# Causal attention with relative bias: heads' values in one PSUM bank, division moved behind the weighing, four-row score tiles, next job's bias and maximum ahead of norm work

## The reference, cut to what matters

```python
q, k, v = heads_split(x @ Wq), heads_split(x @ Wk), heads_split(x @ Wv)
q = q * cos + _rotate_half(q) * sin
k = k * cos + _rotate_half(k) * sin
scores = jnp.einsum('bhqd,bhkd->bhqk', q, k) / sqrt(HD) + bias
scores = jnp.where(causal, scores, jnp.float32(-1000000000.0))
attn = jax.nn.softmax(scores, axis=-1)
ctx = jnp.einsum('bhqk,bhkd->bhqd', attn, v)
return ctx.transpose(0, 2, 1, 3).reshape(b, s, d) @ Wo
```

## Time and profile before

| | us |
|---|---|
| median of 3 runs (2390.05 to 2390.89) | 2390.89 |
| the profiled execution's own time | 2393.39 |
| its span | 2391.5 |
| PE busy | 2271.0 (95%) |
| DVE busy | 1760.3 (74%) |
| POOL busy | 1595.7 (67%) |
| ACT busy | 1380.1 (58%) |

### The profile page before, as it was taken

The page is one execution under the profiler, slowest core; times in us unless marked ns, Lnnn a source line. Parts: engine busy times, 40 slices in busy tenths (PEclk is TensorE's granted clock), DMA queues, the critical chain, the costliest instruction groups (busy, mean ns, idle before and its releaser), DMA issues.

```text
span 2391.5 us, 81638 instructions
## 1 busy us (share of the span) xinstructions
PE 2271.0 (95%) x34944; PEld 1573.3 (66%) x34944; DVE 1760.3 (74%) x2707; ACT 1380.1 (58%) x2778; POOL 1595.7 (67%) x931
## 2 busy tenths in 40 slices
PE   7789999999999999999999999999987888889998
PEld 5456666666666666666666666666655666657776
DVE  3678888888888788878887888888846888853332
ACT  2256666666666666666666666666644666643442
POOL 1298888988898889888988888898833132201111
PEclk9799999999999999999999999999987999989999
DMA  4011112111221112211121112111121000000000
GB/s 116 3 38 36 32 34 67 44 34 31 60 53 33 32 36 60 52 32 36 44 59 40 36 32 61 49 37 32 33 77 48 1 1 2 1 1 1 5 5 9
DMA packets 77303, 83.91 MB, mean 35 GB/s; under 512 B 24964, under 2 KB 48786, under 8 KB 76946
## 3 DMA queue, kind: packets, MB, share of 16 engines
q1 hardware_dynamic: 76946, 78.70, 12.9%
HBM read 26.56 MB, written 1.07 MB: 12 GB/s over the span
## 4 chain that ended last, share of the span: by engine, by line
PE 63%; DVE 19%; issue 10%; ACT 5%; POOL 2%; SPq 0%; ACTq 0%; DMA 0%; POOLq 0%; DVEq 0%
PE bank L565 8%; PE bank L646 7%; PE bank L658 6%; DVE n L1288 5%; PE lnbank L586 4%; PE obank L635 4%; ACT qk L950 3%; PE bank L576 3%; PE obank L627 3%; PE sbank L602 3%; PE bank L666 3%; PE obank L612 3%; PE obank L868 2%; PE sbank L868 2%; PE sbank L791 2%
## 5 line engine op out<-in xcount | busy, mean ns | idle before, releaser
L1281 DVE TENSOR_TENSOR qk<-bank,tab 128x1024 f32<-128x1024 f32 x384 | 468.8, 1221 | 193.6 <-ACT qk L950 193.5
L1601 POOL TENSOR_TENSOR rn<-n2m,cst 128x16 f32<-128x16 f32 x192 | 562.5, 2930 | 16.0
L1597 POOL TENSOR_TENSOR qk<-qk 128x1024 f32<-128x1024 f32 x192 | 454.4, 2366 | 157.9 <-DVE qk L1281 157.9
L950 ACT ACTIVATE qk<-bank 128x512 f32<-128x512 f32 x384 | 226.9, 591 | 313.8 <-PE bank L565 313.8
L565 PE MATMUL bank<-wqk,xs 128*128 128x512 f32 x768 | 404.9, 609 | 1.4 <-ACT qT L968 0.7
L1605 POOL TENSOR_TENSOR qk<-qk,rn 128x1024 f32<-128x1024 f32 x192 | 365.1, 1902 | 28.2 <-POOL rn L1601 0.9
L576 PEld LDWEIGHTS bank<-cst,qk 128*128 128x128 f32 x1536 | 191.7, 141 | 215.1 <-issue 170.7
L576 PE MATMUL bank<-cst,qk 128*128 128x128 f32 x1536 | 232.3, 274 | 10.8 <-POOL qk L1605 10.7
L1288 DVE TENSOR_REDUCE n<-qk 128x16 f32<-128x1024 f32 x192 | 232.1, 1209 | 0.0
L1609 POOL TENSOR_TENSOR lnr<-lnv,cst 128x2 f32<-128x2 f32 (+1 forms) x76 | 54.2, 713 | 248.4 <-DVE lnv L1165 248.4
L586 PE MATMUL lnbank<-wv,xs 128*64 128x512 f32 x768 | 207.2, 618 | 0.0
(11 more groups left out here) (362 smaller groups left out, 4239.3 us busy)
## 6 DMA issues: line engine op xcount, KB each, us to landing
vp<-vp SPq DMA_DIRECT2D x672, 65.0 KB, 2.0
wqk<-in_L_ffn_Wqkv SPq DMA_DIRECT2D x24, 256.0 KB, 3.6
wv<-in_L_ffn_Wqkv SPq DMA_DIRECT2D x6, 512.0 KB, 4.2
wo<-in_L_ffn_Wo SPq DMA_DIRECT2D x6, 512.0 KB, 4.2
xs<-Z SPq DMA_DIRECT2D x48, 64.0 KB, 2.4
xs<-Z SPq DMA_DIRECT2D x48, 63.8 KB, 2.1
vp<-in_L_ffn_w SPq DMA_DIRECT2D x1, 2048.0 KB, 13.2
mw<-in_L_ffn_w SPq DMA_DIRECT2D x8, 256.0 KB, 6.8
```

The lines of the kernel that those rows point to most:

```text
L1281: tt(qk[:, both, :].rearrange("p o (h d) -> p o h d", d=DH), heads(bank[c % 2][:, :]).unsqueeze(1).broadcast_to([P, 2, PAIRS, DH]), table. ...
L1597: tt(direct, direct, swapped, ALU.add).then_inc(sum_done, 1)
L1601: tt(rn[:, m % 2, :], n2m[:, :], const("mhalf"), ALU.pow).then_inc(rn_done, 1)
```

## The change

- **Jobs**: a group y of three jobs now takes the heads y, y+4, y+8 and y+12. Their queries and keys lie in four different sets of 32 rows, so `qm` is masked only within 32 rows (four copies instead of 16, double-buffered), and the scores of a whole group are taken at once (`scores3`): eight products of 32 rows each, one bank of `quad` per set.
- **DVE**: `shift3` does addition and negated extreme in one instruction per head (scores are stored negated, and the exponential has scale -1), and it handles job m+1 in slot m, ahead of that slot's norm work.
- **Division**: exponentials are transposed and weighed undivided; row sums are kept for the batch (`dn`), inverted once (`invert`), spread over the features with a copy and two transposes (`spread_inverses`), and multiplied to the weighed values (`divide3`).
- **Values**: `placed` takes 32 columns around a head's 8 values (zeros beside them), so that 4 heads add up in one set of 32 rows: all 16 heads in one bank of 256 columns, in the order of features. The output projection is one product.
- **Order**: `sh` and `px` have three buffers; a step has 12 slots, the next batch's first group follows in slot 11; only the last step has four more. ACT does its norm work of slot m-1 in slot m, between its exponentials and its copy.
- **Loads**: bias in a buffer of its own, loaded behind layer 0 of the windowed stage; `mw2` in the memory of `kT` and `tab`; the output weights in one transfer, without zeroing.

```diff
-JOBS = [job for n in range(0, H, 4)
-        for job in ((0, range(n, n + 4)), (1, range(n, n + 2)), (1, range(n + 2, n + 4)))]
+JOBS = [job for y in range(4)
+        for job in ((0, range(y, H, 4)), (1, range(y, H // 2, 4)), (1, range(H // 2 + y, H, 4)))]
...
             layer(0, True, False)
+            sp.dma_start(bias[:, :, :], bass.AP(relu_dram.ap().tensor, 0, [[1, P], [384, H], [1, S]])).then_inc(rel_in, 16)
...
-            for half in range(2):
-                sp.dma_start(bias[half], bass.AP(relu_dram.ap().tensor, half * PAIRS * 384, [[1, P], [384, PAIRS], [1, S]]))\
-                    .then_inc(rel_in, 16)
...
             def out3(b):
-                pe.wait_ge(s3["ot"], 2 * b + 2)
-                for g in range(4):
-                    mm = nc.tensor.matmul(lnbank[:, 0:S], s3wo[:, g, :], s3ot[:, g, :], start=(g == 0), stop=(g == 3))
-                mm.then_inc(s3["y"], 1)
+                pe.wait_ge(s3["ot"], b + 1)
+                nc.tensor.matmul(lnbank[:, S:2 * S], s3wo, s3ot, start=True, stop=True).then_inc(s3["y"], 1)
...
+            def scores3(b, odd, y):
...
+                wait(pe, s3["mx"], NJ * b + 3 * y)
+                for r in range(2):
                     w = P * (r + 1)
+                    for g in range(4):
+                        rows = slice(WIN * g, WIN * g + WIN)
+                        mm = nc.tensor.matmul(quad[:, g, P * r:P * r + w], qm[rows, odd, y, r * P:r * P + P],
+                                              s3k[odd][rows, 0:w], start=True, stop=True)
+                mm.then_inc(s3["full"], 1)
+
+            def turn3(n):
+
+                pe.wait_ge(s3["px"], n + 1)
+                wait(pe, s3["pts"], n)
+                for q in range(4):
+                    mm = nc.tensor.transpose(bank[2][:, q * P:q * P + P], s3px[n % 3][:, q * P:q * P + P], ident)
+                mm.then_inc(s3["ptf"], 1)
...
+            def weigh3(n):
...
+                for kb in range(r + 1):
+                    for x, h in enumerate(heads):
+                        row, q = WIN * (h // 4), x * (r + 1) + kb
+                        mm = nc.tensor.matmul(bank[b % 2][row:row + WIN, lo:lo + P], placed(b % 2, kb, h),
+                                              pT[:, n % 2, q * P:q * P + P], start=(m == 0), stop=(y == 3 and kb == r),
+                                              skip_group_check=True)
...
             def step3(b, odd, next_batch, batch_before):
                 u = 3 * b + (LN_S3 + 1)
-                for m in range(NJ + 3):
-                    attend(b, odd, m)
+                for m in range(NJ if next_batch else NJ + 4):
+                    n = NJ * b + m
+                    if 2 <= n <= NJ * B + 1:
+                        turn3(n - 2)
+                    if m in (2, 5, 8):
+                        scores3(b, odd, m // 3 + 1)
+                    if m == NJ - 1 and next_batch:
+                        scores3(b + 1, 1 - odd, 0)
+                    if 3 <= n <= NJ * B + 2:
+                        weigh3(n - 3)
...
+                    if m == 3 and batch_before:
+                        spread_inverses(b - 1)
...
             def step3(b, odd, next_batch, batch_before):
                 u = 3 * b + (LN_S3 + 1)
-                for m in range(NJ + 3):
-                    attend(b, m)
+                for m in range(NJ if next_batch else NJ + 4):
+                    n = NJ * b + m
+                    if m < NJ:
+                        exps3(b, m)
+                    if batch_before:
+                        finish(b - 1, m - 1, u + 2 if next_batch else u)
                     if next_batch:
-                        prepare(b + 1, 1 - odd, m, u if batch_before else LN_S3 + 2)
...
+                        prepare(b + 1, 1 - odd, m - 1, u if batch_before else LN_S3 + 2)
+                    if m == 3 and batch_before:
+                        take_raw(b - 1)
...
+                    if 2 <= n <= NJ * B + 1:
+                        take_turned3(n - 2)
...
+            def shift3(b, m):
...
+                for x, h in enumerate(heads):
+                    last = nc.vector.tensor_tensor_reduce(out=s3sh[n % 3][:, x * w:x * w + w], in0=quad[:, h // 4, P * r:P * r + w],
+                                                          in1=bias[:, h, S - w:S], scale=-1.0, scalar=3e38, op0=ALU.add,
+                                                          op1=ALU.min, accum_out=mx[:, n % 3, x:x + 1])
+                last.then_inc(s3["mx"], 1)
...
+            def divide3(b):
+
+                dve.wait_ge(s3["rdw"], b + 1)
+                wait(dve, s3["y"], b)
+                tt(s3ot.rearrange("p (r t) -> p r t", r=2), s3raw.rearrange("p (r t) -> p r t", r=2),
+                   bank[b % 2][:, 0:S].rearrange("p (r t) -> p r t", r=2)[:, :, ::-1], ALU.mult).then_inc(s3["ot"], 1)
...
-                for m in range(NJ + 3):
-                    if m < NJ:
-                        attend(b, m)
-                    if 1 <= m <= NJ:
-                        normalise3(b, m - 1)
+                for m in range(NJ if next_batch else NJ + 4):
+                    if m < NJ - 1:
+                        shift3(b, m + 1)
+                    if m == NJ - 1 and next_batch:
+                        shift3(b + 1, 0)
+                    if m == 2 and batch_before:
+                        invert(b - 1)
```

More of the change, by code:

```diff
@@ L167, in build @@
         w1t = rotf[:, 512:1024]
-        mw2 = sb("mw2", [P, NE, 4, DIM])
+        bias = sb("bias", [P, H, S])
         sh = sb("sh", [P, 2, 512])
@@ L835, in _ @@
             step3(B - 1, 1, False, True)
-            for slot in range(9, 13):
-                finish(B - 1, slot, LN_S4 - 1, False)
+            for slot in range(8, 12):
+                finish(B - 1, slot, LN_S4 - 1)
             pe.wait_ge(ld_gate, 64)
@@ L1057, in finish @@
                 if slot == 9:
-                    act.wait_ge(s3["y"], b + 1)
-                    nc.scalar.copy(s3y, lnbank[:, 0:S]).then_inc(s3["ys"], 1)
-                if slot == 10:
                     ln_sq_act(S, u)
-            def attend(b, m):
-                if 2 <= m <= NJ + 1:
-                    act.wait_ge(s3["ptf"], NJ * b + m - 1)
-                    wait(act, s3["pv"], NJ * b + m - 3)
-                    nc.scalar.copy(pT[:, m % 2, :], bank[2][:, :]).then_inc(s3["pts"], 1)
-                if m < NJ:
-                    r, heads = JOBS[m]
-                    w = P * (r + 1)
-                    act.wait_ge(s3["mx"], NJ * b + m + 1)
-                    wait(act, s3["ptf"], NJ * b + m - 1)
-                    for n in range(len(heads)):
-                        last = nc.scalar.activation(px[:, m % 2, n * w:n * w + w], sh[:, m % 2, n * w:n * w + w], ACT.Exp,
-                                                    bias=mx[:, m % 2, n:n + 1], accum_out=dn[:, m % 2, n:n + 1])
-                    last.then_inc(s3["px"], 1)
@@ new lines, in exps3 @@
+            def exps3(b, m):
+                n = NJ * b + m
+                r, heads = JOBS[m]
+                w = P * (r + 1)
+                act.wait_ge(s3["mx"], n + 1)
+                wait(act, s3["ptf"], n - 2)
+                if m == 0:
+                    wait(act, s3["rdn"], b - 1)
+                for x, h in enumerate(heads):
+                    last = nc.scalar.activation(s3px[n % 3][:, x * w:x * w + w], s3sh[n % 3][:, x * w:x * w + w], ACT.Exp,
+                                                bias=mx[:, n % 3, x:x + 1], scale=-1.0,
+                                                accum_out=dn[:, b % 2, H * r + h:H * r + h + 1])
+                last.then_inc(s3["px"], 1)
```

214 lines of the change are left out of this document (101 added, 113 removed).

## The result

The kernel after takes 2307.32 us (median of 4 runs, 2304.07 to 2308.62) against 2390.47 for the kernel before, measured beside it: ratio 0.9651, 95% interval 0.9634 to 0.9668, so 83 us less where 49 were forecast. The profiled execution took 2308.0 us; its span is 2306.2.

A forecast was written before the change was run, and what follows sets the result against it. Bound: a serial walk through PE, DVE and ACT, per job before, per three-job group after. Savings of 41.5 (six middle steps), 7.4 (first) and 0.5 us (last) make 49.4: 2393.4 to 2344.0, adjusted to 2342; range 2310 to 2376.

The forecast's parts named there:

- The new walk: Second attention: serial path through PE, DVE and ACT once per group of three jobs, 7.44 us without norm work.
- The moved loads: Bias, weight tables and small loads issued elsewhere: forecast zero effect, up to 12 us if a spreading were late.
- ACT's wait for the maximum: Sign: ACT's largest idle time, before a four-head job's exponentials, ended by DVE, four times a step, about 2 us each.
- Scores of a group: PE's eight score products per group: 1.3 us, half the serial time, plus 0.15 until DVE starts; bounds 0.65 and 2.6.
- Fused operation: DVE's addition and maximum in one instruction per head: 0.38 us for 128 elements, 0.51 for 256.
- the copy between the exponentials: ACT's copy between four-head and two-head exponentials on each group's walk: 0.62 us.
- norm work on the walk: ACT's norm copies and squares, plus PE's projections outlasting the walk: 2.6 us a step.
- The first step: First of the second attention's eight steps: 7.4 us saved, with less norm work and a clock of 0.88 before.
- the last with its tail: Last step, 37.0 us with its drain against 35.97, and 1.5 us back from the projection: 0.5 us saved.
- Cheaper parts: Rival: scores overlap fourfold and the accumulator costs nothing, 2303 us, or some 2322 with only one; chance 25%.
- the double gain: Both cheap parts at once, fourfold score overlap and free accumulator output, 2303 us; left out of the range.
- norms and rotary, unchanged: DVE's norm and rotary work per step in the second attention: 8.0 us, taken as the same after the change.

The follow-up runs named there:

- e7: Changed kernel with one more 512-wide DVE addition in each slot of the six middle steps, behind the slot's other work: 2310.4 us.
- e14: Changed kernel with PE computing each group's eight score products twice, into the same places: 2329.1 us.
- e1: Changed kernel with all score products reading the first 32 rows, so none overlap and the output differs: 2402.35 us.
- e15: Changed kernel with each job's fused DVE operations done once more, ahead, into a scratch buffer: 2346.8 us.
- e5: Changed kernel with ACT's norm work issued in its own slot, not one slot later: 2353.1 us.
- e6: Changed kernel with DVE's shift of the next job behind the slot's norm work, not ahead of it: 2398.7 us.
- e13: Changed kernel with both order edits, those of e5 and e6, together: 2407.2 us.
- e9: Kernel of e6 with two unneeded 256-column PE products ahead of the weighing in nearly every slot: 2428.0 us.
- e10: Changed kernel with PE's scores ahead of the turn (2289.6 us), plus unneeded PE products behind the weighing in the first step's slots 3 to 11: 2295.0 us.

## Why the prediction was right and wrong

**Right: the bound and its kind.** The new walk, one per group of three jobs, and its members are in the trace as written: 32 waits of ACT for the maximum, 32 of DVE for scores. e7 shows that DVE's sum doesn't bind, e14 that scores stand on the walk one to one. The moved loads cost nothing: the stage starts 0.3 us earlier. No low clock remains between batches in the steady steps. ACT's wait for the maximum comes once a group as foretold, but is 1.2 us and not 2.

**Wrong: the size of two terms.** The forecast gave the walk 7.44 us per group without norm work; it is 6.26, 1.18 less. Two terms are 1.08 of that.

- *Scores of a group*: "I take half of the serial time, 1.3 us, plus 0.15 until DVE starts". Measured: 0.94 us, and 1.00 to DVE's start, 0.45 less. The step that failed is the choice between bounds: I discounted overlap because the row with small tiles had two row groups. Four row groups overlap 3.1-fold (0.94 against 2.88 us in e1), and the second pass of e14, 0.65 us, is just the forecast's bound for four at a time. The Trainium skill (TensorEngine Tiling (Array Packing), section Theoretical Speedup) gives up to 4x at 32 rows; the runs come near it, and not to half of the serial time.
- *Fused operation*: "I take ScalarE's extra of 0.18, as the nearest row: 0.38 and 0.51". Measured 0.21 and 0.34, the lower bound of 0.20 and 0.33. Shift to exponentials is 0.97 us, not 1.6: 0.63 less. The Trainium skill (VectorE: DVE Perf Modes, section Two Vector instructions with no wait between them) counts the accumulator's output as a second instruction; it is one in the trace, 0.08 us, but it starts with the next operation, and the pitch shows no time for it. A price carried over from another engine was the mistake.

The doubling runs say what an error in each term weighs: a microsecond of scores 1.0 (21.8 over 20.8), and one of the four-head job 1.0 in the two groups of e15 that are otherwise undisturbed. The 39.5 us of e15 as a whole are 1.5 times 32 times 0.84, but the two-head jobs were doubled too, and the clock fell; they are no weight of the one term.

1.08 us in each of four groups is 26 of the 29 us missed in six middle steps; the rest came from the copy between the exponentials (0.47 between starts, not 0.62) and from norm work on the walk, 2.3 us a step as against 2.6. The first step gave 12.2 in place of 7.4, the last with its tail 2.4 in place of 0.5. Together 36 us.

Both errors lay on the same side, and the prediction held them together as its rival *Cheaper parts*, "2303", at 25%; the measured 2307 is that case. The range left it out by its own words ("leaving out the double gain"). The two terms weren't independent coin throws of a quarter: each time I had chosen a dearer value, though the trace of before held a row for the near bound, for DVE and the earlier trace rows for PE.

**Not seen: what the order is worth.** The walk treated "ahead of norm work" as a place in a sum. e5, e6 and e13 cost 46, 91 and 100 us, far beyond the operations that change places, because each one queues a short operation behind a chain over three in-order engines (the waits are shown with e5 and e6), and the clock falls with the waits. A forecast made for a version with the order half done would have missed by those amounts. How much of e5's 46 us is clock and how much waiting wasn't separated by a run.

## What to carry to other kernels

In a pipeline of in-order engines, price a moved operation by what the operations now ahead of it wait for, not by their duration, and undo or add such moves together with the one that feeds them. Where a new operation's cost is bounded from both sides, take the row of the same engine (pitch by element count) rather than a behaviour of another engine, and if two terms are chosen cautiously, keep the case in which both are cheap in the range. Once the walk was short, swapping two neighbours on PE gave 18 us more, until PE was 95% full; the two further reorderings tried lost 12 and 14. Products added only to fill PE's waits raised the clock and still lost, 29 and 5 us.

## What the runs showed of the hardware

**An addition of DVE under a product of GpSimd.** In the kernel before, a residual addition of 256 columns took 0.43 us alone and 1.37 while GpSimd masked the queries (DVE and GpSimd, 1968 to 1981 us):

```profile
1968.50 4.23 POOL L1655 TENSOR_TENSOR qk<-qk,cst 128x1024 f32<-128x1024 f32 x2
...
1969.61 1.37 DVE L1428 TENSOR_TENSOR X<-X,lnt 128x256 f32<-128x256 f32 x1
...
1980.97 0.43 DVE L1401 TENSOR_TENSOR X<-X,lnt 128x256 f32<-128x256 f32 x1
```

The six of L1428 in the middle steps averaged 1.37 us, and the twelve of L1417 0.91. After, with a quarter of the masking, no row is stretched (stage 1800 to 2100 us by form):

```profile
L1449 DVE TENSOR_TENSOR qk<-qk 128x256 f32<-128x256 f32 x16 | 6.8, 425 | 0.5
L1460 DVE TENSOR_TENSOR X<-X,lnt 128x256 f32<-128x256 f32 x8 | 3.4, 425 | 0.3
```

That is 6 x 0.94 + 12 x 0.49 = 11.5 us of DVE time, a gain that the prediction took for nothing ("norms and rotary, unchanged"); what of it was on the path wasn't tried. The Trainium skill (SBUF — State Buffer, section Who interferes with whom) says that only these two engines' shared port contends, as an exclusive lock; the addition of 1.37 us, begun under the first of two products of 2.1 us, ended 0.4 us behind that one's end, which fits; no run here isolates it.

**A start flag beside a running sum.** In e9 the added products were begun with a start flag in columns that nothing uses, in a bank whose other columns were being summed, and the output changed (relative error 0.46); in e10 they went to a bank with no open sum, and it didn't. The Trainium skill (PSUM — Partial Sum Buffer, section The four PSUM rules) says that a starting product clears the written marks of the whole 2 KiB bank, so that later parts overwrite; the two outputs agree with it. e9 is used for its time alone.
